# A cross-attention and FFN kernel on one core: LN2's rows turned by VectorE in 32x32 blocks and carried through DRAM, row statistics turned one tile sooner

## The reference

```python
x = x + xattn(layernorm(x), ctx_1024)     # LN1, similarity, softmax, weighted context, product with W_qv + b_qv
x = x + ffn(layernorm(x))                 # LN2 and the feed-forward part

def layernorm(x): return (x - mean(x)) / sqrt(var(x) + 1e-5)      # over the 512 features
def ffn(x):
    hidden = x @ W1 + b1                                            # 512 -> 2048
    imag = w_imag * sin(theta + hidden * 0.1)
    q = hidden + (cos(theta) * w_real + sin(theta) * w_imag) * imag * 0.1
    return relu(q) @ W2 + b2                                        # 2048 -> 512
```

## Time and profile before

| what | value |
|---|---|
| median of three runs | 1956.96 us (1955.17 to 1958.2) |
| profiled execution, its own time | 1955.15 us |
| its span, first to last instruction | 1953.3 us |
| mean granted TensorE clock | 0.998 of full |
| PE busy | 1938.4 us, 99% |
| PE's weight loads busy | 1585.8 us, 81% |
| DVE busy | 1379.2 us, 71% |
| ACT busy | 990.4 us, 51% |
| POOL busy | 408.4 us, 21% |
| DMA | 397.63 MB, mean 204 GB/s |

### The profile page before, as it was taken

One profiled execution on the slowest core, in us unless ns is written; L12 is line 12 of the kernel. 1 busy time (PEld: TensorE's weight loads), 2 busy tenths in 40 slices (PEclk: granted clock), 3 DMA queues, 4 the chain that ended last, 5 costly groups with the idle time before them and its releaser, 6 DMA issues.

```text
span 1953.3 us, 24524 instructions
## 1 busy us (share of the span) xinstructions
PE 1938.4 (99%) x8709; PEld 1585.8 (81%) x8709; DVE 1379.2 (71%) x2377; ACT 990.4 (51%) x1676; POOL 408.4 (21%) x834
## 2 busy tenths in 40 slices
PE   8999999999999999999999999999999999999999
PEld 7778788888888888888888888888888888888887
DVE  7888786766777676776766867667776667767554
ACT  5574645536365363644636455363653636446343
POOL 1223121131211212112121211312122121221210
PEclk9999999999999999999999999999999999999999
DMA  8587857577574875757667475774748757576463
GB/s 258 175 282 244 263 160 238 171 229 226 161 224 141 254 233 164 212 175 226 203 202 222 158 232 166 233 228 159 222 149 253 225 172 213 170 225 189 151 216 119
DMA packets 144279, 397.63 MB, mean 204 GB/s; under 512 B 22380, under 2 KB 35416, under 8 KB 142238
## 3 DMA queue, kind: packets, MB, share of 16 engines
q0 software_dynamic: 83568, 304.29, 49.9%
q1 hardware_dynamic: 60446, 91.74, 15.6%
q10 hardware_dynamic: 144, 0.04, 0.0%
HBM read 355.50 MB, written 38.30 MB: 202 GB/s over the span
## 4 chain that ended last, share of the span: by engine, by line
PE 93%; DVE 3%; ACT 2%; issue 1%; DMA 0%; SPq 0%; DVEq 0%; ACTq 0%
PE acc L521 18%; PE acc L523 17%; PE acc L522 17%; PE hid L521 11%; PE hid L523 11%; PE hid L522 11%; PE mis L607 1%; PE acc L529 1%; PE mis L529 1%; PE acc L530 1%; PE mis L530 1%; PE mis L523 1%; PE mis L521 1%; PE mis L522 1%; DVE ph L1225 0%
## 5 line engine op out<-in xcount | busy, mean ns | idle before, releaser
L521 PE MATMUL hid<-T,w1s 128*128 128x512 f32 x1024 | 403.6, 394 | 3.3 <-ACT h L884 3.3
L521 PE MATMUL acc<-ws,act 128*128 128x512 f32 x1024 | 402.8, 393 | 2.2 <-DVE ws L1082 1.5
L523 PE MATMUL hid<-T,w1s 128*128 128x512 f32 x1024 | 399.8, 390 | 0.0
L522 PE MATMUL hid<-T,w1s 128*128 128x512 f32 x1024 | 399.8, 390 | 0.0
L523 PE MATMUL acc<-ws,act 128*128 128x512 f32 x1024 | 399.2, 390 | 0.0
L522 PE MATMUL acc<-ws,act 128*128 128x512 f32 x1024 | 398.7, 389 | 0.0
L890 ACT ACTIVATE act<-h 128x512 fp32r<-128x512 f32 x256 | 161.9, 633 | 353.7 <-DVE h L1215 332.3
L1223 DVE TENSOR_SCALAR kk<-ph 128x512 f32<-128x512 f32 x256 | 108.7, 425 | 323.0 <-ACT ph L881 323.0
L881 ACT ACTIVATE ph<-hid,hbias 128x512 f32<-128x512 f32 x256 | 175.6, 686 | 279.6 <-PE hid L523 279.2
L1590 POOL DMA_DIRECT2D ws<-w2x_dram x240 | 127.3, 531 | 513.6 <-PE acc L523 504.2
L521 PEld LDWEIGHTS hid<-T,w1s 128*128 128x128 f32 x1024 | 192.9, 188 | 44.9 <-issue 4.1
(11 more groups left out here) (192 smaller groups left out, 2710.9 us busy)
## 6 DMA issues: line engine op xcount, KB each, us to landing
w1s<-w1x_dram POOLq DMA_DIRECT2D x240, 512.0 KB, 4.4
ws<-w2x_dram POOLq DMA_DIRECT2D x240, 512.0 KB, 4.4
ws<-wqx_dram POOLq DMA_DIRECT2D x56, 512.0 KB, 4.7
full<-in_x_turned SPq DMA_DIRECT2D x15, 1024.0 KB, 4.8
out_x<-X SPq DMA_DIRECT2D x15, 1024.0 KB, 4.7
X<-in_x SPq DMA_DIRECT2D x14, 1024.0 KB, 8.5
w_raw<-in_L_ffn_W SPq DMA_DIRECT2D x32, 256.0 KB, 3.7
w1x_dram<-w1s POOLq DMA_DIRECT2D x16, 512.0 KB, 4.4
```

The costliest lines, as they stand in the source:

```text
L521: pe.matmul(dst, w_hi, m_hi, start=start, stop=False)
L522: pe.matmul(dst, w_hi, m_lo, start=False, stop=False)
L523: mm = pe.matmul(dst, w_lo, m_hi, start=False, stop=stop)
```

## The change

LN2's turn leaves TensorE. VectorE's `transpose` turns each 32x32 block of a tile of normed rows in itself (`block_turn`) and writes the blocks to `ctx_raw`, whose context rows are used up by then. SP stores `ctx_raw` (1 MB, 8 KB from each partition) to `block_dram`, waits for that store (`t2_st`), and loads it back by four transfers of 256 KB, each to 32 partitions of `T`'s low half (pieces of 2 KB in DRAM). ScalarE makes the high parts from there (`blocks_high`) and VectorE the low parts in place (`blocks_low`), four of 128x512 each. The rows of `T` now stand in another order, four groups of 128 for each feature chunk, so `hidden` reads its moving operand in four runs of 128, and `phase_and_hidden` reads `hid` in runs of 32 and puts the rows back in order. `turn_stats` and `stat_rows` stand ahead of the first `second` of f = 12 instead of behind the third.

```diff
+    block_dram = nc.dram_tensor("block_dram", [2, P, 4, D], F32).ap()
...
+            def block_moves(n):
+                sp.wait_ge(xb2, RT * n)
+                sp.dma_start(block_dram[n % 2], ctx_raw[:]).then_inc(t2_st, 16)
+                sp.wait_ge(t2_st, 16 * n)
+                by_feature = block_dram[n % 2].rearrange("(i a) m k -> m a i k", i=G)
+                for m in range(G):
+                    sp.dma_start(T_run[n % 2][32 * m:32 * m + 32, 1].bitcast(F32), by_feature[m]).then_inc(t2_in, 16)
...
                     if f == (NA + 3 if first else NA + 2):
                         spread_stats(n + 1)
+                    if f == NA + 3:
+                        block_moves(n)
...
+                        m = [T_run[par][:, k, :, c * P:(c + 1) * P] for k in range(2)]
...
+                    if f == NA + 2 and n + 1 < B:
+                        turn_stats(n + 1)
                     if f == NA + 2 and not last:
                         second(b, NA - LAG, False)
                         second(b, NA - LAG + 1, False)
...
-                    if f == NA + 2 and n + 1 < B:
-                        turn_stats(n + 1)
-                    if f == NA + 3:
-                        tr_second(n, 0)
-                        tr_second(n, 1)
-                    if f == NA + 4:
-                        tr_second(n, 2)
-                        tr_second(n, 3)
...
+            def blocks_high(n, i):
+                sc.wait_ge(t2_in, 16 * G * n)
+                nc.scalar.copy(T_run[n % 2][:, 0, i], T_run[n % 2][:, 1, i].bitcast(F32)).then_inc(t2_hi, 1)
...
-                nc.scalar.activation(ph[:, f % 2], hid[:, f % 2], ACT.Identity, bias=hbias[:, f:f + 1],
+                nc.scalar.activation(by_rows(ph[:, f % 2], b), by_groups(hid[:, f % 2], b), ACT.Identity, bias=hbias[:, f:f + 1],
...
                     if f == NA + 4:
-                        turned_high(n, 2, pn, tr2, t2_hi)
-                        turned_high(n, 3, pn, tr2, t2_hi)
+                        for i in range(G):
+                            blocks_high(n, i)
...
+            def block_turn(n, t):
+                ve.wait_ge(xn2, RT * n + t + 1)
+                ve.transpose(blocks[:, :, :, t].rearrange("p m c r -> p c m r"),
+                             xin[:, t % 2].rearrange("p (c m r) -> p c m r", c=C, m=G)).then_inc(xb2, 1)
+
+            def blocks_low(n, i):
+                ve.wait_ge(t2_hi, RT * n + i + 1)
+                low(T_run[n % 2][:, 1, i], T_run[n % 2][:, 1, i].bitcast(F32), T_run[n % 2][:, 0, i]).then_inc(t2_lo, 1)
...
+                    if f == NA + 5 and not last:
+                        for i in range(G):
+                            blocks_low(n, i)
                     reduce_phase(b, f)
...
+                    if f == NA + 2 and not last:
+                        norm_second(n, 0)
+                        block_turn(n, 0)
                     if (f > 0 or not first) and not early:
                         relu_low(g - 1, (f - 1) % FT)
...
+                    if f == NA + 2:
+                        for t in range(1, RT):
+                            norm_second(n, t)
+                            block_turn(n, t)
```

More of the change, by code:

```diff
@@ L330, in xattn_ffn, with by_rows, by_groups @@
         x0n = w0_sb
+        G = P // 32
+        blocks = ctx_raw[:].rearrange("p a d -> p (a d)").rearrange("p (m c t r) -> p m c t r", m=G, c=C, t=RT)
+        T_run = [T[:, q].rearrange("p a c r -> p a (c r)").rearrange("p a (i k) -> p a i k", i=G) for q in range(2)]
+        def by_rows(cols, b):
+            return cols if b == 0 else cols.rearrange("p (t i r) -> p t i r", t=RT, i=G)
+        def by_groups(cols, b):
+            return cols if b == 0 else cols.rearrange("p (i t r) -> p t i r", t=RT, i=G)
         g_view = g_raw.rearrange("p (c j) -> p c j", c=C)
@@ L577, in hidden @@
                 for c in range(C):
-                    three(hid[:, f % 2], w[:, 0, c], w[:, 1, c], T[:, par, 0, c], T[:, par, 1, c],
+                    if b == 0:
+                        m, dst = [T[:, par, k, c] for k in range(2)], hid[:, f % 2]
+                    else:
+                        m = [T_run[par][:, k, :, c * P:(c + 1) * P] for k in range(2)]
+                        dst = hid[:, f % 2].rearrange("p (i k) -> p i k", i=G)
+                    three(dst, w[:, 0, c], w[:, 1, c], m[0], m[1],
                           c == 0, c == C - 1, hid_done if c == C - 1 else None)
@@ L634, in sim_rows @@
                 pe.wait_ge(simt_done, n + 1)
+                need(pe, srow_done, n)
                 for t in range(RT):
@@ L1015, in body @@
                     phase_and_hidden(b, f)
+                    if f == NA + 2 and n + 1 < B:
+                        stat_rows(n + 1)
                     if first and f < FT - 3:
@@ L1046, in body @@
                         max_exponentials(n)
-                    if f == NA + 2 and n + 1 < B:
-                        stat_rows(n + 1)
                     if f == NA - 1:
@@ L1461, in body @@
                         spread_low(n, 3, pn)
-                    if f == NA + 3 and not last:
-                        norm_second(n, 0)
-                        norm_second(n, 1)
-                    if f == NA + 4 and not last:
-                        norm_second(n, 2)
-                        norm_second(n, 3)
+                    if f == NA + 5 and not last:
+                        for i in range(G):
+                            blocks_low(n, i)
                     reduce_phase(b, f)
```

16 lines of the change are left out of this document (4 added, 12 removed).

## The result

The changed kernel takes 2040.36 us (median of four runs, 2036.37 to 2044.48) against 1956.24 us before (now a median of four as well): a ratio of 1.0433, interval 1.0419 to 1.0446. It is 4.3% slower, where I had forecast 0.8% faster. The profiled execution took 2044.48 us, its span is 2042.7 us.

A forecast was written before the change was run, and what follows sets the result against it. TensorE's own instructions, 93% of the chain of waits, were taken as the bound. 1955.15 less 26.4 (transposes) plus 10.6 (body 0) plus 0 (fourteen bodies) gave 1939.4; with the runs' median 1.8 above, 1941 us, range 1931 to 1958.

The forecast's parts named there:

- The transposes' 26.4 us: TensorE: dropping LN2's sixteen transposes a body, 1.76 us, saves 26.4 us over fifteen bodies; upper end 31.2.
- The moved statistics: TensorE: `turn_stats` ahead of f = 12's first `second` costs what it did, with no wait.
- their rival: Hidden matmuls: reading four runs of 128 slows each by 7 ns, 20 us in all, time 1961; chance 0.08.
- The block transposes: VectorE: each block transpose takes 0.64 us, bounds 0.50 and 1.28.
- the deadline: Middle body: `t2_lo` must be there when TensorE starts `hidden(b + 1, 0)`, at 1024.0 in the new kernel.
- the 3.2 us from the copies to `t2_lo`: Middle body, ScalarE's four copies and VectorE's low parts: `t2_lo` comes 3.2 us after the copies start.
- The term is **0**, its upper end 3.5 a body: Fourteen middle bodies: TensorE doesn't wait for `t2_lo`; at most 3.5 us a body if store and loads each take 8.5.
- The store's "4.8": Middle body: the 1 MB store of the blocks lands 4.8 us after issue, bounds 4.7 and 8.5.
- the loads' "4.75": Middle body: the four 256 KB loads have landed after 4.75 us, at 1016.9; upper end 8.5.
- the carry is late in every body: Rival, ahead of `hidden(b + 1, 0)`: TensorE waits every body, 2.2 us giving 1972, 3.5 giving 1990; chance 0.14.
- half rate: Rival: 32-partition loads land 3.5 us later, lengthening only body 0's wait by 3.5; time 1945; chance 0.13.
- TensorE waits **10.6 us**, once: Ahead of body 1's first matmul: body 0's late carry makes TensorE wait 10.6 us, ends 8.3 and 15.8.

The follow-up runs named there:

- run 2: Changed kernel with neither the blocks' store nor the four loads issued, so LN2's values are missing: 1930.66 us, ratio 0.9873 to the kernel before; span 1927.6.
- run 1: Kernel before the change with only `turn_stats` and `stat_rows` moved to their new places: 1955.68 us, ratio 0.9995.
- run 11: Changed kernel with POOL holding the weights' loads of tile 13 and later until the four block loads have landed, not in body 0: 2073.55 us, ratio 1.0603.
- run 7: Changed kernel with the weights' loads in bodies 1 to 15 cut to 64 KB from 512, output not computed: 1945.2 us, ratio 0.9947.
- run 3: Changed kernel with each of the four loads written to all 128 partitions, exchange between partition groups left out: 1997.98 us, ratio 1.0216.
- run 6: Changed kernel with body 0's store issued between two raw tile loads and its block loads behind the last: 2031.98 us, ratio 1.0391.
- 5: Changed kernel with unused filler matmuls ahead of the next body's first hidden matmul, 15 a body, 60 in body 0: 2034.75 us, ratio 1.0408.
- after: The changed kernel itself, against the kernel before: 2040.36 us, ratio 1.0433.
- 4: Changed kernel with sixteen transfers straight from `ctx_raw` to `T`, without the store to DRAM: 2010.63 us, ratio 1.0282.
- 8: Changed kernel with block loads 0 and 1 issued by SP, 2 and 3 from ScalarE's queue: 2004.94 us, ratio 1.0254.
- run 14: As run 13, with the block loads to partitions 64 to 127 issued from ScalarE's queue: 1951.45 us, ratio 0.9978.
- run 13: Changed kernel with run 6's order in body 0, POOL holding weights from tile 13's second W2 load until the blocks land: 1960.08 us, ratio 1.0018.

## Why the prediction was wrong, point by point

**Right, and shown.** The transposes' 26.4 us (run 2: 0.7 off). The moved statistics (run 1). The reads in four runs (run 2; their rival falls). The block transposes: 0.71 us each against 0.64. The issue of the store, 16.7 us ahead of the deadline, and the 3.2 us from the copies to `t2_lo` (3.3).

**The step that failed**: "The term is **0**, its upper end 3.5 a body", for the fourteen middle bodies. It was 4.7, 66.3 us in all. Below it stand two prices that were too small. The store's "4.8" took 7.3 on average over bodies 1 to 14, and the loads' "4.75" took 10.8 to the last landing, so 18.1 in place of 9.6. That is 8.5 us later; I had worked out that TensorE begins to wait at 3.9 us later, and 8.5 - 3.9 is 4.6. So the budget and the point where it breaks were placed rightly, and only the two landings were wrong. The rival "the carry is late in every body" is what happened, with a price above its upper end, and its chance of 0.14 was too low.

Why these prices were too small is what the runs show. By itself the carry takes 4.0 + 7.6 = 11.6 us (11), 2.0 over my 9.6 and within the 3.9; beside the weights' loads the store takes 3.3 more and the loads 3.2.

- *Company.* I took prices of whole transfers that ran "beside such loads at a mean of 204 GB/s". A mean over the span says nothing of the microseconds in question. I had read 99% at 301 GB/s in the 6 us before, and put it into the upper end alone. Light weights (7) take every wait from the middle bodies, and holding the weights back for long enough (11) lands the store in 3.9.
- *Narrow loads.* The rival "half rate" had the mechanism right, and its size was not too small: I priced it as 3.5 us and said that it alone doesn't reach TensorE. It does not (7, 11): without company the loads take 7.6, less than 4.75 + 3.5, and beside the weights' loads narrowness adds 2.0 us to the landing in a middle body (3). But on top of the company that is 36.5 us of waiting. I weighed each cause against the margin by itself, never both together.
- *Body 0.* "TensorE waits **10.6 us**, once", with 15.8 as upper end: 16.8. The place and the reason (SP's order) were right (6 takes 10.1 us off), the two landings were again too short.

**What was missing altogether**: a price for the clock. The sum had no term for what TensorE does after a wait. It is most of the 32.7 us that are left, and some 25.6 lie in the hidden matmuls. Keeping TensorE at work brings them back to 394 ns (5), which shows the cause. It isn't the same in each run. The table has the span over run 2's and what is left of it without the waits. The last two columns come from the traces' record of the granted clock: how many of the fifteen starts of a body have the lower level at them or just behind them, and how long TensorE works at that level in bodies 1 to 15, outside the waits.

| run | waits us (times) | span over run 2's | left over | starts at the lower level | us at that level |
|---|---|---|---|---|---|
| after | 83.1 (15) | 115.1 | 32.0 | 12 | 55 |
| 6 | 67.5 (15) | 96.0 | 28.5 | 13 | 53 |
| 4 | 53.2 (15) | 85.6 | 32.4 | 13 | 62 |
| 8 | 51.7 (15) | 70.0 | 18.3 | 7 | 30 |
| 3 | 46.6 (14) | 65.4 | 18.8 | 8 | 33 |
| 7 | 14.7 (1) | 15.1 | 0.4 | 1 | 4 |

So it is not the length of the waits that decides between 18 and 32, but how many of them the lower level follows: half of the last column is 28, 27, 31, 15, 16 and 2. Apart from run 7 (see there) that leaves 1 to 4 us, of which the opening, up to 2.4 us longer than in run 2, is a part. In the changed kernel a body without that level works 0.6 to 1.0 us longer than in run 2, one with 3.1 to 3.4 us of it 1.7 to 2.2 longer, and one with 5.0 to 7.9 us of it 2.2 to 4.8 longer; only body 1 is no longer, since run 2 has short waits there. Why the level follows one wait and not another stays open: in run 6 it follows one of 2.11 us and not one of 3.13.

**Also open.** Where most of the 6.5 us lie by which run 14 stays above floor and waits (1.4 are the opening), how two queues gain beside the weights' loads, and why run 14 is faster than run 13. A wide exchange that is also complete wasn't found: run 3 leaves the exchange out, so it bounds what wide loads would bring and is no version to use.

## What to carry to other kernels

When a step goes off the bounding engine onto DMA, price the transfers by what is in flight in those very microseconds, not by the landing times of the same shape elsewhere: here a 1 MB store landed in 3.9 us alone and in 7.3 beside the weights' loads. Add up the causes of lateness before holding them against the margin. Price a wait on TensorE that comes back in every round above its length: here it was 0.6 to 1.0 us where the clock stayed up and 1.7 to 4.8 where it fell, for waits of 2.5 to 8.9. If a carry must compete with prefetches, hold these for the transfer and no longer: the short hold took 72 us off (run 13 against run 6), the hold that began ahead of the tile's first load added 33 (run 11 against the changed kernel). Even so, the whole effort ended 0.2% below the kernel before.

## What the runs showed of the hardware

- Four loads that write 32 neighbouring partitions each, all in flight, move 213 to 238 GB/s at full DMA share (the changed kernel, runs 11, 13 and 14). With the same 2 KB pieces to 128 partitions the engines move 347 to 374 (run 3, weights' loads among them), and the store from 128 partitions, by itself, moves 350 at a share of 0.84 (run 11). So the narrow ones have some 0.6 of the rate. The direction agrees with the Trainium skill's page SBUF — State Buffer, Door 1: The DMA port swizzle, by which such a transfer reaches half of the ports. Nothing here tells why it is a little more than half. Neither four in flight nor two issuing queues make up for it.
- The same 1 MB store lands in 3.9 us with no weights' load in flight (run 11) and in 7.3 beside them, both medians. The four narrow loads take 7.6 and 10.8 us to the last landing, on average.
- Within 1 us behind a wait of 3.56 us TensorE's hidden matmuls come to start 0.43 us apart instead of 0.23, and take 0.63 instead of 0.39: the lower of its two levels, 1.2 GHz. The granted clock of these 3 us is 0.50. In run 6 the lower level follows a wait of 2.11 us, but not one of 3.13.
- Sixteen issues of 64 KB between partitions took SP's queue 10.2 us, 0.64 each, where four of 256 KB take 1.75, 0.44 each.
